# A graph network's second edge stage: maps with the turned features as the stationary operand, and the weighting of the values on VectorE

## What is computed

```python
ms = src_s[edge_src] + dst_s[edge_dst]
mv = src_v[edge_src] + dst_v[edge_dst]
w1, w2, w3, w4, w5 = split(h @ rw3 + roff)
ds = concat([w1 * ms, w4 * (mv . Y1) / SQ3])
dv = concat([w2 * ms * Y1, w3 * mv, w5 * cross(mv, Y1) / SQ2])
ls, lv = ds @ lin_ws + lin_bs, einsum('nud,uk->nkd', dv, lin_wv)
alpha, vs, vv = ls[:, :64], ls[:, 64:], lv
a = einsum('ehk,hk->eh', smooth_leaky(alpha), alpha_dot)
a = exp(a - segment_max(a, edge_dst)[edge_dst])
ns = segment_sum(vs * a, edge_dst)
nv = segment_sum(vv * a, edge_dst)
```

## Time and profile before

| | |
|---|---|
| median of 3 runs | 10097.84 us (10063.66 to 10109.07) |
| the profiled execution | 10064.59 us, of it the profile's span 10062.5 us |
| PE busy | 8731.8 us (87%) |
| DVE busy | 7958.4 us (79%) |
| POOL busy | 7733.9 us (77%) |
| ACT busy | 4874.1 us (48%) |
| granted TensorE clock, mean | 0.935 |

### The profile page before, as it was taken

The page is one execution under the profiler, slowest core; times in us unless marked ns, Lnnn a source line. Parts: engine busy times, 40 slices in busy tenths (PEclk is TensorE's granted clock), DMA queues, the critical chain, the costliest instruction groups (busy, mean ns, idle before and its releaser), DMA issues. The chain is left out here.

```text
span 10062.5 us, 191932 instructions
## 1 busy us (share of the span) xinstructions
PE 8731.8 (87%) x34728; PEld 5186.5 (52%) x34728; DVE 7958.4 (79%) x15008; ACT 4874.1 (48%) x9073; POOL 7733.9 (77%) x4771
## 2 busy tenths in 40 slices
PE   0788888888888889999999699999999999999588
PEld 0444444444444423222222477777777777777233
DVE  3177777777777668888888699999999999999455
ACT  0176666666666611111111355555555555555255
POOL 4378888888888878888888588888888888887331
PEclk5599999999999989999999799999999999999699
DMA  5588888888888799999999366666666666665222
GB/s 205 177 161 173 165 165 167 164 170 166 165 165 169 142 225 228 223 231 228 228 232 224 85 144 143 140 142 146 144 141 141 144 145 144 141 142 133 59 69 54
DMA packets 1232080, 1618.01 MB, mean 161 GB/s; under 512 B 218498, under 2 KB 1007501, under 8 KB 1175885
## 3 DMA queue, kind: packets, MB, share of 16 engines
q1 hardware_dynamic: 755862, 1273.87, 46.2%
q0 software_dynamic: 475584, 338.58, 26.5%
HBM read 1533.80 MB, written 444.07 MB: 197 GB/s over the span
## 5 line engine op out<-in xcount | busy, mean ns | idle before, releaser
L1932 POOL DMA_INDIRECT e_m<-TS,e_at x1568 | 2582.3, 1647 | 529.2 <-issue 462.4
L442 POOL DMA_INDIRECT sums<-e_total,e_place x1568 | 2505.7, 1598 | 573.6 <-DMA sums<-e_total,e_place 314.2
L579 PE MATMUL ps<-e_win,e_pick 128*128 128x448 f32 x3136 | 1335.9, 571 | 155.5 <-DVE e_u L476 106.5
L579 PEld LDWEIGHTS ps<-e_win,e_pick 128*128 128x128 f32 x3136 | 620.9, 203 | 919.6 <-issue 835.2
L2255 ACT ACTIVATE e_dT<-ps 128x512 f32<-128x512 f32 x1176 | 660.1, 596 | 485.6 <-PE ps L2129 353.2
L1094 POOL TENSOR_TENSOR n_zv<-n_zv,n_ast 128x1536 f32<-128x1536 f32 x200 | 752.1, 3761 | 160.3 <-DMA n_zv<-in_x_groups 148.3
L2255 ACT ACTIVATE e_oT<-ps 128x512 f32<-128x512 f32 x784 | 468.6, 598 | 645.6 <-PE ps L2157 283.8
L1299 PE MATMUL ps<-n_z,w_uss 128*64 128x512 f32 x1600 | 745.8, 610 | 23.8 <-DVE n_z L1142 22.9
L742 DVE SCALAR_TENSOR_TENSOR r_y<-ps,w_rb,r_rstd 128x512 f32<-128x512 f32 x394 | 295.4, 750 | 583.6 <-issue 537.9
L1916 POOL TENSOR_TENSOR e_val<-e_val 128x640 f32<-128x640 f32 x392 | 667.0, 1702 | 101.1 <-ACT e_val L2232 101.1
L1098 POOL TENSOR_TENSOR n_zv<-n_zv 128x512 f32<-128x512 f32 x400 | 689.4, 1723 | 36.8 <-POOL n_zv L1094 0.4
(11 more groups left out here) (437 smaller groups left out, 19530.3 us busy)
## 6 DMA issues: line engine op xcount, KB each, us to landing
e_win<-T SPq DMA_DIRECT2D x1568, 168.0 KB
n_z<-in_x_groups SPq DMA_DIRECT2D x400, 512.0 KB
n_zv<-in_x_groups SPq DMA_DIRECT2D x800, 192.0 KB
TOT<-e_tot SPq DMA_DIRECT2D x392, 352.0 KB
e_row<-in_src_rows SPq DMA_DIRECT2D x98, 1024.0 KB
e_local<-LR SPq DMA_DIRECT2D x196, 512.0 KB
e_row<-in_dst_rows SPq DMA_DIRECT2D x98, 1024.0 KB
e_win<-TD SPq DMA_DIRECT2D x1568, 60.0 KB
```

Source lines behind the costliest of these rows:

```text
L442: pool.indirect_dma_start(sums[c], bass.IndirectOffsetOnAxis(ap=place[:, r % 4, c:c + 1], axis=0), total[:, r % 4, c, 0:MSG0], None, compu ...
L579: pe.matmul(g[:, c, :], pick[:, p, R * c:R * c + R], win[:, s, c, :], start=True, stop=True).then_inc(spread, 1)
L1932: pool.indirect_dma_start(m_[:, r % 4, c, :], None, TS, bass.IndirectOffsetOnAxis(ap=at[:, gp, col:col + 1], axis=0), compute_op=ALU.add). ...
```

## The change

1. *Maps.* `map_scalars` and `map_vectors` take 128 columns of `dT` (the turned features of one tile) as the stationary operand and the weights as the moving one, 128 columns wide. The result has edges on the partitions at once. Scalars go to PSUM bank 4, vectors to bank 5. The scalar map stands behind `turn(i, 1)` and waits, beside its input, for ScalarE's reads of group i-1 and for the first instruction of VectorE's `results` of group i-1 (`silued`); the vector map stands behind the first totals and waits for the third copy and for `freed`.
2. *Turn back* is gone, with `oT` and ScalarE's two copies to it.
3. *VectorE's results* begin with the product with alpha, and the order of the rest is changed.
4. *Weighting* moves from POOL to VectorE, to the start of each group's stream, six groups late.
5. *Tops.* `tops_down` stands at the end of PE's group, behind both maps and both totals. `weigh_up` moves on ScalarE from the scan group to the next one, behind its far copies.
6. On ScalarE `results` follows the third `keep` of the same group.

The diff, cut to its core; left out are the same edits to counts and the matching lines ahead of and behind the loop:

```diff
@@ -1778,17 +1777,18 @@
...
         w4 = ps[0:R, 0:2, :].rearrange("r b (c x) -> r (b c) x", c=2)
-        out4 = ps[0:R, 4:6, :].rearrange("r b (c x) -> r (b c) x", c=2)
+        scalar_out4 = ps[0:R, 4, :].rearrange("r (c x) -> r c x", c=GT)
+        vector_out4 = ps[0:R, 5, :].rearrange("r (c x) -> r c x", c=GT)
         tot2 = ps[0:R, 6, :].rearrange("r (c x) -> r c x", c=2)[:, :, 0:ROW]
 
-        alpha4, scalars4 = out4[:, :, 0:S], out4[:, :, S:128].rearrange("r c (h x) -> r c h x", x=8)
-        vectors4 = out4[:, :, 128:256].rearrange("r c (h x) -> r c h x", x=16)
+        alpha4, scalars4 = scalar_out4[:, :, 0:S], scalar_out4[:, :, S:128].rearrange("r c (h x) -> r c h x", x=8)
+        vectors4 = vector_out4.rearrange("r c (h x) -> r c h x", x=16)
 
...
         def bank(i, j):
-            return 2 + (7 * i.r + j) % 2
+            return 2 + (5 * i.r + j) % 2
 
...
@@ -1906,16 +1906,6 @@
...
             def _(pool):
-                def weighted(i, back):
-
-                    j = i.r - back
-                    slot, gp = j % STEPS, j % STEPS // 4
-                    gate(pool, k)
-                    pool.wait_ge(exped, i.uses(2, j // 4 + 1))
-                    u = val[:, gp, 4 * (slot % 4):4 * (slot % 4) + 4].rearrange("r c (h x) -> r (c h) x", x=SEG)
-                    pool.tensor_tensor(u[:, :, 1:SEG], u[:, :, 1:SEG], bc(u[:, :, 0], SEG - 1, 2), ALU.mult
-                                       ).then_inc(u_ready, 1)
-
                 def body(t):
...
@@ -2004,24 +1990,36 @@
...
                     dve.wait_ge(outs, i.n(2, 2))
+                    s3 = silu[:, p].rearrange("r c (h x) -> r c h x", h=HEADS)
+                    dve.scalar_tensor_tensor(out=silu[:, p], in0=silu[:, p], scalar=1.5, in1=alpha4, op0=ALU.add, op1=ALU.mult
+                                             ).then_inc(silued, 1)
+                    gate(dve, k)
+                    dve.wait_ge(mapped, i.n(2, 2))
                     for x in range(3):
...
                     last.then_inc(by_y, 1)
-                    s3 = silu[:, p].rearrange("r c (h x) -> r c h x", h=HEADS)
-                    dve.scalar_tensor_tensor(out=silu[:, p], in0=silu[:, p], scalar=1.5, in1=alpha4, op0=ALU.add, op1=ALU.mult
-                                             ).then_inc(silued, 1)
+                    gate(dve, k)
+                    dve.wait_ge(silued, i.n(2, 1))
+                    dve.tensor_tensor(silu[:, p], silu[:, p], bc(W["ad"][0:R, :], GT, 1), ALU.mult).then_inc(silued, 1)
                     gate(dve, k)
...
                     gate(dve, k)
-                    dve.wait_ge(silued, i.n(2, 1))
-                    dve.tensor_tensor(silu[:, p], silu[:, p], bc(W["ad"][0:R, :], GT, 1), ALU.mult).then_inc(silued, 1)
-                    gate(dve, k)
                     dve.wait_ge(silued, i.n(2, 2))
                     dve.tensor_reduce(values(i)[:, :, :, 0], s3, AX.X, ALU.add).then_inc(logit, 1)
+
+                def weighted(i):
+
+                    j = i.r - 6
+                    slot, gp = j % STEPS, j % STEPS // 4
+                    gate(dve, k)
+                    dve.wait_ge(exped, i.uses(2, j // 4 + 1))
+                    u = val[:, gp, 4 * (slot % 4):4 * (slot % 4) + 4].rearrange("r c (h x) -> r (c h) x", x=SEG)
+                    dve.tensor_tensor(u[:, :, 1:SEG], u[:, :, 1:SEG], bc(u[:, :, 0], SEG - 1, 2), ALU.mult
+                                      ).then_inc(u_ready, 1)
 
...
@@ -2056,6 +2054,8 @@
...
                         more = not (isinstance(t, int) and t == PASSES - 1 and r == STEPS - 1)
+                        if not i.before(6):
+                            weighted(i)
                         if more:
...
@@ -2124,7 +2126,7 @@
...
                     else:
-                        pe.wait_ge(kept, i.n(5, j - 1))
+                        pe.wait_ge(kept, i.n(3, j - 1))
                     for c in range(GT):
...
@@ -2146,25 +2148,28 @@
...
                     gate(pe, k)
-                    pe.wait_ge(kept, i.n(5, 2))
-                    pe.matmul(ps[:, bank(i, 5), :], W["la"][:].rearrange("u a h x -> u (a h x)"), dT[:, 0, :], start=True, stop=True
-                              ).then_inc(turned, 1)
+                    pe.wait_ge(kept, i.n(3, 1))
+                    if not i.before(1):
+                        gate(pe, k)
+                        pe.wait_ge(outs, i.n(2))
+                        gate(pe, k)
+                        pe.wait_ge(silued, i.n(2, -1))
+                    for c in range(GT):
+                        last = pe.matmul(scalar_out4[:, c], dT[:, 0, R * c:R * c + R],
+                                         W["la"][:].rearrange("u a h x -> u (a h x)"), start=True, stop=True)
+                    last.then_inc(mapped, 1)
 
...
                     gate(pe, k)
-                    pe.wait_ge(kept, i.n(5, 3))
-                    pe.matmul(ps[:, bank(i, 6), :], W["lb"][:].rearrange("u h x -> u (h x)"), dT[:, 1, :], start=True, stop=False)
-                    pe.matmul(ps[:, bank(i, 6), :], W["lc"][:].rearrange("u h x -> u (h x)"), dT[:, 2, :], start=False, stop=True
-                              ).then_inc(turned, 1)
-
-                def turn_back(i, j):
-                    gate(pe, k)
-                    pe.wait_ge(kept, i.n(5, 4 + j))
-                    if j == 0 and not i.before(1):
+                    pe.wait_ge(kept, i.n(3, 3))
+                    if not i.before(1):
                         gate(pe, k)
...
                     for c in range(GT):
-                        last = pe.transpose(out4[:, c, 128 * j:128 * j + 128], oT[:, j, R * c:R * c + R], I[:])
+                        pe.matmul(vector_out4[:, c], dT[:, 1, R * c:R * c + R], W["lb"][:].rearrange("u h x -> u (h x)"),
+                                  start=True, stop=False)
+                        last = pe.matmul(vector_out4[:, c], dT[:, 2, R * c:R * c + R],
+                                         W["lc"][:].rearrange("u h x -> u (h x)"), start=False, stop=True)
                     last.then_inc(mapped, 1)
...
@@ -2184,28 +2189,23 @@
...
                         if i.plus(3).within():
-                            spread_out(i.plus(3), 0, far2(i, 0), (far_kept, 5) if i.before(1) else (kept, i.n(5, -1)))
-                        if not i.before(1):
-                            turn_back(i.plus(-1), 0)
-                        if i.plus(3).within():
-                            spread_out(i.plus(3), 1, far2(i, 1), (far_kept, 6) if i.before(1) else (kept, i.n(5)))
-                        if not i.before(1):
-                            turn_back(i.plus(-1), 1)
+                            spread_out(i.plus(3), 0, far2(i, 0), (far_kept, 5) if i.before(1) else (kept, i.n(3, -1)))
+                            spread_out(i.plus(3), 1, far2(i, 1), (far_kept, 6) if i.before(1) else (kept, i.n(3)))
                         if not (isinstance(t, int) and t == PASSES - 1 and r == STEPS - 1):
...
                         turn(i, 1)
+                        map_scalars(i)
+                        turn(i, 2)
                         if not i.before(6):
                             totals(i, 0)
-                        turn(i, 2)
+                        map_vectors(i)
+                        if not i.before(6):
+                            totals(i, 1)
                         if r % 4 == 1 and not i.before(5):
                             tops_down(i)
-                        map_scalars(i)
-                        if not i.before(6):
-                            totals(i, 1)
-                        map_vectors(i)
                         if r % 4 == 0 and not i.before(4):
...
@@ -2247,12 +2245,11 @@
...
                     gate(act, k)
-                    act.wait_ge(turned, i.n(5, j + 1))
+                    act.wait_ge(turned, i.n(3, j + 1))
                     if not i.before(1):
...
                         act.wait_ge(mapped, i.n(2))
-                    to = dT[:, j, :] if j < 3 else oT[:, j - 3, :]
-                    act.activation(to, ps[:, bank(i, 2 + j), :], ACT.Copy).then_inc(kept, 1)
+                    act.activation(dT[:, j, :], ps[:, bank(i, 2 + j), :], ACT.Copy).then_inc(kept, 1)
 
...
@@ -2268,7 +2265,7 @@
...
                     gate(act, k)
-                    act.wait_ge(mapped, i.n(2, 2))
+                    act.wait_ge(mapped, i.n(2, 1))
                     if not i.before(2):
...
@@ -2284,26 +2281,21 @@
...
                             keep_far(i.plus(3), 1, far2(i, 1))
-                        if not i.before(1):
-                            results(i.plus(-1))
+                        if r % 4 == 2 and not i.before(6):
+                            weigh_up(i.plus(-1))
                         keep(i, 0)
                         keep(i, 1)
+                        keep(i, 2)
+                        results(i)
                         if not i.before(6):
                             keep_totals(i, 0)
-                        keep(i, 2)
```

(18 more changed lines are left out.)

## The result

| | before | after |
|---|---|---|
| median | 10100.19 us (10063.66 to 10109.07) | 10430.76 us (10410.75 to 10442.62) |
| profiled execution | 10064.59 us | 10437.57 us |

Ratio 1.0334, 95% interval 1.0307 to 1.0360: **3.3% slower**. The forecast was 10150 us, slower by 0.7%, with a range to 10280. The sign was right, the size was not.

The account below looks back on a forecast made before the run. POOL was taken as the bound, 36.95 us for four groups; VectorE's 34.48 plus 3.09 of waiting gave 37.57, +61 us over 98 times, with 12 more for PE waits and 5 less drain about +70: 10150 us, range 9880 to 10280.

Parts of the forecast that it names:

- The lock: VectorE's e_q, held until POOL's weighting ends, would fall from 1.777 to 0.68 us; 4.4 us in four groups.
- Weighting on VectorE: The weighting moved to VectorE would cost it 0.73 us a group.
- VectorE's plain group: VectorE's work in a group without scans would be 8.16 us; four groups with scans and shift 34.48 us.
- POOL: Without the weighting, POOL's need would fall to 7.80 us a group and it would stop being the bound.
- The wait: VectorE's shift would wait for PE's tops: a 4.92 us chain after alpha's product, less 1.83 us of VectorE work.
- Rival 5: The lock on e_q stays if gathers also hold it: 1.10 us a group, +430, 10580 us; chance 0.03.
- Rival 3: Weight loads for the narrow maps make PE the bound: 10.9 us a group, 10750 us, halfway 10240; chance 0.05.
- it stands still 3.09 us in every fourth group: VectorE idle before the shift in scan groups, 3.09 us, 98 times, taking four groups from 34.48 to 37.57 us.
- end of alpha's product to scalar map: On PE, the scalar map would start 0.06 us after VectorE has read alpha.
- PE's group: PE's plain group would take 8.35 us, fitting beside VectorE's 8.16 only just, easily in scan groups.
- Exp and the copy of the tops: Moved to the next group on ScalarE, they would stay covered: nothing counted, 72 us if uncovered.
- Rival 4: PE idles up to 2.3 us, its clock falls and the chain behind alpha doubles: +390, 10540 us; chance 0.07.

Follow-up runs that it names:

- experiment 2: The kernel before with only the weighting moved from POOL to the start of VectorE's group, six groups late: 10006.84 us, ratio 0.9912.
- experiment 1: The changed kernel with the transposition of the tops put ahead of the scalar map on PE: 10363.34 us, ratio 1.0256.
- Experiment 6: Experiment 5 with both totals moved earlier on PE, and ScalarE's copies with them: 9995.12 us, ratio 0.9918.
- experiment 7: The changed kernel with only the totals moved earlier, tops and exponential left late: 10265.15 us, ratio 1.0191.
- experiment 8: Experiment 5 with SP's store of the totals one group later: 10120.79 us, ratio 1.0056.
- experiment 9: The changed kernel with only SP's store of the totals one group later: 10354.76 us, ratio 1.0286.
- experiment 3: The changed kernel with the weighting back on POOL, eight groups late; maps, order and tops as changed: 10633.94 us, ratio 1.0538.
- experiment 11: Experiment 6 with the weighting back on POOL: 10255.54 us, ratio 1.0187.
- experiment 10: Experiment 6 with SP's store of the totals one group later: 9970.77 us, ratio 0.9896.
- experiment 12: Experiment 10 with VectorE's weighting put behind the products of the next group: 9968.77 us, ratio 0.9906.
- experiment 5: Experiment 1 with ScalarE's exponential (`weigh_up`) moved to the end of the scan group: 10289.49 us, ratio 1.0221.

## Why the prediction was right and wrong

**Right.** *The lock.* e_q went to 0.682 us, and experiment 2 shows that its removal is worth more than the weighting costs VectorE. *Weighting on VectorE*: 0.82 us a record and 0.74 from its start to the next one's (7528.95 to 7529.69), 0.73 forecast. *VectorE's plain group*: 8.16 us forecast, 7529.69 - 7521.50 = 8.19 found. *POOL* got its slack. *The wait*: the shift stands still in each scan group, released by the tops; experiment 1 moved it. Rival 5 (the lock stays) fell by the e_q row. Rival 3 (weight loads bind) fell too: the scalar map takes 0.99 us and the vector map 1.89, 2.88 against 2.58, 1.12 times. The figures of the Trainium skill's page "TensorE: Matmul & The Clock Gate", section Back-to-back issue gap, make an estimated 2.5 times; f32 in this kernel does not follow them. Experiment 6 has all 24 narrow records and is faster than before.

**Wrong: "it stands still 3.09 us in every fourth group".** It was 4.75 us on the mean. Two scan groups of the changed kernel show why. First VectorE and PE in the shorter one:

```profile
7512.04 0.40 DVE L1994 SCALAR_TENSOR_TENSOR e_silu<-e_silu,ps 128x256 f32<-128x256 f32 x1
...
7512.93 1.16 PE L2158 MATMUL ps<-w_la,e_dT 128*128 128x128 f32 x8 [0.25 <-issue]
7513.92 0.60 PE L2131 MATMUL ps<-ident,e_d 128*128 128x128 f32 x4
7514.36 0.74 PE L2145 MATMUL ps<-e_val,e_q 128*128 128x168 f32 x4
7515.21 0.49 PE L2169 MATMUL ps<-w_lb,e_dT 128*128 128x128 f32 x2
...
7517.10 0.74 PE L2145 MATMUL ps<-e_val,e_q 128*128 128x168 f32 x4
7517.67 0.27 PE L2186 MATMUL ps<-ident,e_top 128*128 128x128 f32 x1
...
7518.05 0.43 DVE L2051 TENSOR_TENSOR e_val<-e_val,ps 128x128 f32<-128x128 f32 x1 [3.88 <-PE ps L2186]
```

then the longest one, the first of the next pass:

```profile
7550.98 1.35 PE L2120 MATMUL ps<-e_win,e_pick 128*128 128x160 f32 x8 [1.57 <-DMA e_win<-TD]
...
7553.12 3.08 PE L2106 MATMUL ps<-w_r,e_h 128*128 128x224 f32 x8 [0.80 <-DMA e_h<-H]
...
7553.60 0.41 DVE L1994 SCALAR_TENSOR_TENSOR e_silu<-e_silu,ps 128x256 f32<-128x256 f32 x1
...
7556.00 1.46 PE L2131 MATMUL ps<-ident,e_d 128*128 128x128 f32 x8
...
7558.06 1.15 PE L2158 MATMUL ps<-w_la,e_dT 128*128 128x128 f32 x8 [0.60 <-issue]
...
7563.18 0.44 DVE L2051 TENSOR_TENSOR e_val<-e_val,ps 128x128 f32<-128x128 f32 x1 [7.43 <-PE ps L2186]
```

| step of the chain, us | forecast | shorter | longest |
|---|---|---|---|
| end of alpha's product to scalar map | 0.06 | 0.49 | 4.05 |
| scalar map | 0.86 | 0.99 | 0.99 |
| turn 2 | 0.43 | 0.44 | 0.43 |
| totals, wait for the copy | 0.87 | 0.85 | 0.85 |
| vector map | 1.73 | 1.89 | 1.89 |
| totals | 0.58 | 0.57 | 0.57 |
| tops to VectorE | 0.39 | 0.38 | 0.39 |
| sum | 4.92 | 5.61 | 9.17 |
| VectorE's work beside it | 1.83 | 1.73 | 1.74 |
| wait | 3.09 | 3.88 | 7.43 |

Every length on PE's queue was nearly right. The maps add 0.29 (0.12 us a record, not 0.108), VectorE's shorter work 0.10, and the rest of the 1.66 us lies in the first line, which is 1.35 us on the mean of the 74 waits from 6000 to 9000 us (0.20 to 4.04), while the steps from the scalar map to the tops take 4.74 us in all 74: **the forecast took for granted that PE is ready when VectorE has read alpha**. It added PE's group up to 8.35 us, called that a fit "only just", and gave it no lead to lose. A plain group of PE took 7542.46 - 7533.71 = 8.75 us. In the changed order PE has no lead, and what delays it goes straight into the tops. That it is the order and not the amount of work shows in experiment 7, where the first line is 0.19 us with the same maps. Two delays were not in the text at all:

- *SP's queue.* The forecast counted PE's, VectorE's and ScalarE's order, not SP's. Its waits for the second totals, the largest of SP's in 7000 to 8000 us, before and after:

```profile
SPq L1853 <- ACT e_tot L2266: 65.9, 47, 2.2
```
```profile
SPq L1853 <- ACT e_tot L2263: 132.7, 52, 6.4
```

  The second totals moved behind the vector map, so the store, and the loads of windows and e_h behind it, were issued later. At the loop's head SP stops as well, after and before:

```profile
7540.66 0.42 SPq L1853 DMA_DIRECT2D TOT<-e_tot  x1
7545.80 0.36 SPq L1830 DMA_DIRECT2D e_win<-TD  x1
```
```profile
7523.69 0.01 SPq L1853 DMA_DIRECT2D TOT<-e_tot  x1
7528.28 0.36 SPq L1830 DMA_DIRECT2D e_win<-TD  x1
```

  The stop is 5.1 us after and 4.6 before (5.0 and 4.6 on the mean), and the load behind it goes out 5.2 us ahead of the spreading at 7550.98, which waits for it; the mean is 5.1, where before it was 6.0. That late issue costs time is what experiments 8 and 9 show.
- *The loop's head.* Its cost on VectorE showed as 0.46 us before:

```profile
7528.13 0.56 DVE L1960 TENSOR_TENSOR e_prod<-e_m,yx 128x384 f32<-128x384 f32 x1 [0.39 <-issue]
```

  and in the changed kernel as two stops:

```profile
7538.28 0.83 DVE L2021 TENSOR_TENSOR e_val<-e_val 128x640 f32<-128x640 f32 x1 [1.10 <-issue]
...
7540.88 0.56 DVE L1946 TENSOR_TENSOR e_prod<-e_m,yx 128x384 f32<-128x384 f32 x1 [1.77 <-issue]
```

  2.8 us x 49 is 137 us, a term that the sum had at nothing. The size goes with the weighting's place: 0.46, 1.1 and 1.0 us a pass with it on POOL (before, experiments 3 and 11), 1.9 to 3.1 with it on VectorE (experiments 2, 6, 10, 12 and the changed kernel). My reading is that with it on POOL a part is hidden beside operations held by the lock, so that the 4.4 us of lock in four groups were not all to be had; that this is the reason is argued, not shown by a run.

**"Exp and the copy of the tops: I count nothing"** came true in the sum and was wrong in the reason. It held because the tops were later; once they were early the wait was 3.7 us on the mean in experiment 1, 2.9 in 5 and 1.7 in 8.

**Rival 4 (the clock falls)** came in part. The mean granted clock of the stretch is 0.98, but in short pieces it is lower. From 6000 to 9000 us it fell 36 times to the half level, in the kernel before never; PE stood idle for over 1 us 184 times there, at most 2.76 us, and 95 times before, at most 1.54. Two of the pieces, behind idle times of 1.85 us up to 7525.13 and of 1.57 us up to 7550.98:

```profile
7525.00:7530.00 5.00, 4.87 (x28) 4.90 (x29) 5.00 (x13) 1.62 (x4) 2.25 (x2) 0.66 0.53 92
7552.00:7557.00 5.00, 4.20 (x17) 3.60 (x16) 3.50 (x11) 0.77 (x2) 3.27 (x3) 0.66 0.48 121
```

0.66 over 5 us is a mixture of the full level, 2.4 GHz, and the half, 1.2. In the second stretch the edge weights took 3.08 us, 1.8 times the 1.68 of another group: 1.4 us more on the chain. What all 36 cost isn't shown; experiment 10 has 40 such falls and is faster than the kernel before.

**Open.** Why PE still comes 0.63 us late in experiment 9; how much of the loss the lower clock makes; and what VectorE and SP do at the loop's head, since the profile names nothing that they wait for.

## What to carry to other kernels

On engines with strict order the last item of a queue is as late as everything ahead of it, and this holds for the queue that only issues DMAs: when work is moved, list whose wait stands ahead of the loads. A chain's length is only half of a wait; write down beside it when the engine is ready to begin, and if it has no lead, expect more. Each wait taken away here had another behind it, so test the parts of a change one at a time (the weighting alone gained 0.9% inside a change that lost 3.3%), and then all early places together (experiments 1 and 5 gained little each, under 1% by the ratios; 6 gained 294 us).

## What the runs showed of the hardware that was not expected

- The lock between POOL and VectorE struck different VectorE operations as the order changed, all with two SBUF operands: e_q (1.777 us), and e_cr (1.704 in experiment 11), e_prod and e_cA as well. In the timeline of experiment 11 e_cr begins 0.32 us ahead of POOL's record and still is held till 7508.77, 0.42 after POOL's end. The Trainium skill's page "SBUF — State Buffer", section SBUF: two separate sides, calls the shared port an exclusive lock that goes to the one that starts first. The exclusive part agrees; by the records' starts the first was the one that waited. POOL's record is longer there too, 1.85 us against the 1.26 of one that began alone, so starts in the trace don't tell who held the lock.
- Gathers on POOL don't hold e_q: it stays at 0.68 us beside them.
- Gathers have no fixed time: 1.81 us on the mean in experiment 6 and 1.65 in experiment 12, at nearly the same pace, so that their mean says nothing of a bound here.
- The head of the hardware loop stops VectorE for 1.9 to 3.1 us a pass where it does the weighting, for 0.5 to 1.1 where POOL does, and SP for 4.6 us (before) to 5.4 (experiments 6 and 10). With the first instructions exchanged (experiment 12) the stop on VectorE was no shorter.
